# Fused co-attention and expert kernel: DMA transposes of two or three pieces, six fp16 piece buffers, constant matmuls ahead of the expert blocks, a down block between at the switch

## The reference

```python
c  = layernorm(x)
s  = (c @ w_c + b_c)[:, None] + (ctx @ w_q + b_q)[None, :] + einsum('cd,qd,d->cq', c, ctx, w_cq) + b_cq
a  = softmax(s, axis=1)
att = a @ ctx
b_att = softmax(max(s, axis=1))
q2c = b_att @ c
z  = concat([c, att, c * att, c * q2c]) @ W_l.T + b_l
x  = x + z
# mixture of 8 experts, each row goes to one
n  = layernorm(x)
e  = argmax(n @ wr + br)
x  = x + gelu(n @ w1[e] + b1[e]) @ w2[e] + b2[e]
```

## Time and profile before

| | us |
|---|---|
| median of 3 runs | 235.63 (235.04 to 236.16) |
| the profiled execution's own time | 233.51 |
| its span, first to last instruction | 231.8 |
| TensorE matmul busy | 198.0 (85%) |
| VectorE busy | 180.0 (78%) |
| ScalarE busy | 158.0 (68%) |
| POOL busy | 130.5 (56%) |
| DMA queue of SP, share of 16 engines' span | 93.2% |

### The profile page before, as it was taken

One profiled execution on the slowest core, in us unless ns is written; L12 is line 12 of the kernel. 1 busy time (PEld: TensorE's weight loads), 2 busy tenths in 40 slices (PEclk: granted clock), 3 DMA queues, 4 the chain that ended last, 5 costly groups with the idle time before them and its releaser, 6 DMA issues.

```text
span 231.8 us, 5012 instructions
## 1 busy us (share of the span) xinstructions
PE 198.0 (85%) x1837; PEld 148.7 (64%) x1837; DVE 180.0 (78%) x393; ACT 158.0 (68%) x249; POOL 130.5 (56%) x179
## 2 busy tenths in 40 slices
PE   0298798995999969999999999899993799799970
PEld 0133356663676736776866767789983799789960
DVE  2789997995997994997997998958847447567770
ACT  2750799994799689399699699689432355667630
POOL 4699405999607987505906988654400740037783
PEclk9999999999999988999999999999995579999997
DMA  6999999899999999999989999969992459999200
GB/s 206 382 277 247 192 298 244 182 221 201 262 193 254 226 203 226 267 170 243 245 193 261 209 204 225 212 141 210 237 285 78 146 200 296 370 365 382 71 21 0
DMA packets 141918, 51.25 MB, mean 221 GB/s; under 512 B 121156, under 2 KB 139733, under 8 KB 141894
## 3 DMA queue, kind: packets, MB, share of 16 engines
q1 hardware_dynamic: 140960, 49.56, 93.2%
q0 software_dynamic: 784, 1.38, 1.7%
q10 hardware_dynamic: 150, 0.00, 0.0%
HBM read 10.22 MB, written 3.75 MB: 60 GB/s over the span
## 4 chain that ended last, share of the span: by engine, by line
PE 42%; DVE 22%; DMA 12%; issue 11%; ACT 9%; POOL 3%; DVEq 0%; ACTq 0%; POOLq 0%
DMA PT<-Phl 10%; DVE S L792 5%; PE psX L1075 5%; PE psS L1055 5%; PE psS L1057 5%; PE psS L1056 5%; ACT S L646 5%; DVE Phl L809 4%; PE psO L1075 4%; ACT Phl L661 3%; PE psS L1288 3%; PE psX L1077 3%; POOL out_x L603 2%; PE psS L1274 2%; PE psO L1077 2%
## 5 line engine op out<-in xcount | busy, mean ns | idle before, releaser
L646 ACT ACTIVATE S<-S,negb 128x1024 f32<-128x1024 f32 x48 | 55.0, 1145 | 14.6 <-DVE negb L800 14.6
L792 DVE TENSOR_SCALAR_CACHE_REDUCE S<-psS 128x1024 f32<-128x1024 f32 x48 | 58.2, 1216 | 8.2 <-PE psS L1057 7.7
L809 DVE TENSOR_TENSOR Phl<-S,Phl 128x1024 f16<-128x1024 f32 x38 | 50.9, 1340 | 7.7 <-ACT Phl L661 7.6
L661 ACT CAST Phl<-S 128x1024 f16<-128x1024 f32 x48 | 50.2, 1045 | 6.1 <-DMA PT<-Phl 4.7
L533 POOL TENSOR_TENSOR Phl<-S,Phl 128x256 f16<-128x256 f32 x40 | 26.2, 685 | 48.6 <-ACT Phl L661 48.6
L1055 PE MATMUL psS<-qT,gh 128*128 128x512 f16 x96 | 37.8, 394 | 3.3 <-DVE gl L769 2.7
L1075 PE MATMUL psO<-qn,PT 128*128 128x256 f16 x204 | 37.4, 277 | 2.5 <-DMA PT<-Phl 2.4
L1075 PE MATMUL psX<-qn,PT 128*128 128x256 f16 x204 | 36.4, 273 | 2.6 <-DMA PT<-Phl 2.6
L1056 PE MATMUL psS<-qT,gh 128*128 128x512 f16 x96 | 37.7, 392 | 0.0
L1057 PE MATMUL psS<-qT,gl 128*128 128x512 f16 x96 | 37.7, 392 | 0.0
L1077 PE MATMUL psO<-qn,PT 128*128 128x128 f16 x204 | 36.0, 222 | 0.0
(11 more groups left out here) (239 smaller groups left out, 424.9 us busy)
## 6 DMA issues: line engine op xcount, KB each, us to landing
PT<-wp SPq DMA_DIRECT2D x8, 512.0 KB, 4.9
stageT<-in_ctxT SPq DMA_DIRECT2D x6, 512.0 KB, 7.3
qn<-wp SPq DMA_DIRECT2D x6, 512.0 KB, 6.8
wp<-in_w SPq DMA_DIRECT2D x4, 512.0 KB, 4.8
stageT<-in_w SPq DMA_DIRECT2D x4, 512.0 KB, 4.7
rows_by_expert<-stageT SPq DMA_DIRECT2D x4, 385.5 KB, 5.3
PT<-Phl SPq DMA_TRANSPOSE x48, 4.1
S<-rows_by_expert SPq DMA_DIRECT2D x2, 258.0 KB, 5.6
```

Source lines behind the costliest of these rows:

```text
L646: nc.scalar.activation(slot(t, e), slot(t, e), ACT.Exp, bias=negb[:, t:t + 1], accum_out=Lp[:, t * NG + e:t * NG + e + 1]).then_inc(exp_do ...
L661: nc.scalar.copy(hi, slot(t, e)).then_inc(high_done, 1)
L792: nc.vector.tensor_scalar(out=into, in0=bank(u, n)[:, 0:into.shape[1]], scalar1=1.0 / GS, scalar2=None, op0=ALU.mult, op1=ALU.max, accum_o ...
L809: nc.vector.tensor_tensor(lo, slot(t, e), hi, ALU.subtract).then_inc(low_done, 1)
```

## The change

- A DMA transpose takes a unit of pieces: (0,1), (2,3) and (4,5,tail); for the last tile (0,1), (2,3), (4), (5,tail). The context rows likewise go as (0,1), (2,3), (4,5), (tail). Semaphores `pT_landed` and `qn_landed` count units.
- `Phl` holds all six full pieces and the tail in one row, so a piece has its own place and ScalarE waits in `high` for the unit of the tile before. To fit, the descriptor scratch of POOL's DMAs is 8192 bytes instead of the default (16384).
- On SP's queue, two w1 loads stand ahead of the context transposes; the w2 loads stand behind the last unit of tiles 1 to 4.
- `x_re`: ScalarE copies x early, POOL adds the bias behind its low part of tile 1.
- `fill(n)`: n matmuls of 512 columns on a constant, into a PSUM bank that nobody reads: 2 ahead of the rank matmuls, 12 behind them.
- At b = 6, `down(6)` stands behind `turn(0)` and ahead of `up(8)` instead of behind `turn(1)`.

```diff
-        Phl = sb("Phl", [P, PARTS, 2, GR], F16)
-        Ptail = sb("Ptail", [P, 2, TAILP], F16)
+        PW = 2 * GR
+        Phl = sb("Phl", [P, (NG - 1) * PW + 2 * TAILP], F16)
+        Ptail = Phl[:, (NG - 1) * PW:].rearrange("p (a w) -> p a w", a=2)
...
+        QN_UNITS = ((0, 2), (2, 4), (4, 6), (6, 7))
...
+        def pT_units(t):
+
+            return ((0, 2), (2, 4), (4, 5), (5, NG)) if t == T - 1 else ((0, 2), (2, 4), (4, NG))
...
-            def transpose(t, e):
-
-                wait_low(sp, t, e)
+            def transpose(t, g):
+
+                e0, e1 = pT_units(t)[g]
+                for e in range(e0, e1):
+                    wait_low(sp, t, e)
                 if t > 0:
-                    sp.wait_ge(pv_done, (t - 1) * NG + e + 1)
-                src, _, _, dst = piece(t, e)
-                sp.dma_start_transpose(dst, src).then_inc(pT_landed[e], 16)
+                    sp.wait_ge(pv_done, (t - 1) * NG + e1)
+                end = (NG - 1) * PW + 2 * TAILP if e1 == NG else e1 * PW
+                n = len([j for e in range(e0, e1) for j in tiles(e)])
+                sp.dma_start_transpose(PT[:, 2 * e0 * TW:2 * (e0 * TW + n), :],
+                                       Phl[:, e0 * PW:end]).then_inc(pT_landed[g], 16)
...
-            for k in range(H - 1):
-                load_w1(k)
+            load_w1(0)
+            load_w1(1)
+            for g, (n0, n1) in enumerate(QN_UNITS):
...
+            load_w1(2)
...
+            for t in range(T):
+                for g in range(len(pT_units(t))):
+                    transpose(t, g)
+                if t == 0:
+                    load_w1(H - 1)
+                elif t <= H:
+                    load_w2(t - 1)
...
-            nc.gpsimd.tensor_tensor(x_re, x_sb, blr[:, :].unsqueeze(1).broadcast_to([P, T, D]),
-                                    ALU.add).then_inc(x_re_ready, 1)
...
             low_piece(1, 3)
+            pool.wait_ge(x_kept, 1)
+            pool.wait_ge(late_landed, 16 * NLATE)
+            nc.gpsimd.tensor_tensor(x_re, x_re, blr[:, :].unsqueeze(1).broadcast_to([P, T, D]),
+                                    ALU.add).then_inc(x_re_ready, 1)
...
             deviation(2, H, T)
+            act.wait_ge(qTl_ready, DVE_LOW.index(4) + 1)
+            act.wait_ge(qTl_pool_ready, POOL_LOW.index(5) + 1)
+            nc.scalar.copy(x_re, x_sb).then_inc(x_kept, 1)
...
-                past = t * (NG - 1) + e - PARTS
-                if e == NG - 1 and t > 0:
-                    act.wait_ge(pT_landed[e], 16 * t)
+                if t > 0:
+                    act.wait_ge(pT_landed[pT_unit(t - 1, e)], 16 * t)
...
-                pe.wait_ge(pT_landed[e], 16 * (t + 1))
+                pe.wait_ge(pT_landed[pT_unit(t, e)], 16 * (t + 1 if t < T - 1 or e < 5 else 1))
...
+            filler = ones[:, :].bitcast(F16)
+
+            def fill(n):
+
+                for _ in range(n):
+                    nc.tensor.matmul(psS[2][:, 0:CH], filler[:, 0:P],
+                                     filler.unsqueeze(1).broadcast_to([P, 2, 2 * P]), start=True, stop=True)
...
             linear_c(2)
+            fill(2)
...
             last.then_inc(ranks_in_psum, 1)
+            fill(12)
...
                 if b == E - 2:
                     turn(0)
+                    down(b)
...
                 if b == E - 2:
                     turn(1)
-                down(b)
+                else:
+                    down(b)
```

More of the change, by code:

```diff
@@ L67, in build @@
     SLOTS = 8
-    PARTS = 4
     BANKS = 3
@@ L204, in build @@
         qT_landed = [sem(f"qT_landed{n}") for n in range(NG)]
-        qn_landed = [sem(f"qn_landed{n}") for n in range(NG)]
+        qn_landed = [sem(f"qn_landed{g}") for g in range(4)]
         late_landed = sem("late_landed")
@@ L228, in build @@
         exp_done = sem("exp_done")
-        pT_landed = [sem(f"pT_landed{e}") for e in range(NG)]
+        pT_landed = [sem(f"pT_landed{g}") for g in range(4)]
         high_done = sem("high_done")
@@ L320, in columns, with qn_unit, pT_unit @@
             return buf[:, 0, 0:w], buf[:, 1, 0:w]
+        QN_UNITS = ((0, 2), (2, 4), (4, 6), (6, 7))
+        def qn_unit(n):
+            return min(n // 2, 3)
         def rows_of(n):
-            k = len(tiles(n))
-            buf = qT[:, n, :, :] if n < NG - 1 else qTend[:, :, :]
-            return buf.rearrange("p a w -> p (a w)"), qn[:, 2 * n * TW:2 * n * TW + 2 * k, :]
+            return qn[:, 2 * n * TW:2 * n * TW + 2 * len(tiles(n)), :]
+        def pT_units(t):
+            return ((0, 2), (2, 4), (4, 5), (5, NG)) if t == T - 1 else ((0, 2), (2, 4), (4, NG))
+        def pT_unit(t, e):
+            return [e0 <= e < e1 for e0, e1 in pT_units(t)].index(True)
         def pool_low(t, e):
@@ L349, in bank, with piece @@
             return psS[(u * NG + n) % BANKS]
[L351 to L356, removed]
+        def piece(e):
+            w = cols(e, GR)[1] - e * GR
+            buf = Phl[:, e * PW:(e + 1) * PW].rearrange("p (a w) -> p a w", a=2) if e < NG - 1 else Ptail
+            return buf[:, 0, 0:w], buf[:, 1, 0:w]
         def block_w(b):
@@ L402, in load_w2 @@
                              w2[k * n:(k + 1) * n].rearrange("e (k p) d -> p e k d", p=P)).then_inc(w_landed[H + k], 16)
-            for k in range(H - 1):
-                load_w1(k)
+            load_w1(0)
+            load_w1(1)
+            for g, (n0, n1) in enumerate(QN_UNITS):
+                for n in range(n0, n1):
+                    sp.wait_ge(qTh_ready, n + 1)
+                    if n in DVE_LOW:
+                        sp.wait_ge(qTl_ready, DVE_LOW.index(n) + 1)
+                    else:
+                        sp.wait_ge(qTl_pool_ready, POOL_LOW.index(n) + 1)
+                src = qT[:, n0:n1, :, :].rearrange("p n a w -> p (n a w)") if n1 < NG else \
+                    qTend[:, :, :].rearrange("p a w -> p (a w)")
+                k = sum(len(tiles(n)) for n in range(n0, n1))
+                sp.dma_start_transpose(qn[:, 2 * n0 * TW:2 * (n0 * TW + k), :], src).then_inc(qn_landed[g], 16)
+            load_w1(2)
             for r in (0, 32):
@@ L529, in low_piece @@
                 pool.wait_ge(high_done, t * NG + e + 1)
-                _, hi, lo, _ = piece(t, e)
+                hi, lo = piece(e)
                 for a in range(0, GR, CHUNK):
@@ L1072, in weighted @@
                 n, acc = len(tiles(e)), psA[t % 2]
-                both = rows_of(e)[1].rearrange("p (a j) d -> p a j d", a=2)
+                both = rows_of(e).rearrange("p (a j) d -> p a j d", a=2)
                 for i, j in enumerate(tiles(e)):
```

39 lines of the change are left out of this document (9 added, 30 removed).

## The result

The changed kernel takes 251.31 us (median of 4, 249.56 to 251.76) against 235.66 for the one before: ratio 1.0652, 95% interval 1.0595 to 1.0709. Slower was forecast, by 4.6 us; it is 15.7. The profiled execution took 251.76 us with a span of 250.0, 18.2 more than the span of before, whose execution was 2.1 under its median.

What follows compares the result with a forecast made beforehand. TensorE was taken to set the pace in attention. Attention +5.4, slow landings +1.5, constant matmuls -1.6 and switch -0.7 gave +4.6 us on the median of 235.6: 240.2, rounded to 240, range 231 to 245.

Steps and rivals of the forecast that it cites:

- the wait for the third unit: Attention: pieces 4, 5 and tail land 6.2 us after the tail's low part; TensorE waits 1.1 to 1.4 us each round.
- slow landings: Attention transposes that land late, like one of 6.3 us with no load ahead: +1.5 us, between nothing and 5.
- to the third round: Attention up to 62.18 us: ScalarE's 3.16 us stall goes, waits for pairs come; 1.0 us gained, 1.5 earlier start included.
- third to fifth round: Two attention rounds of 17.9 us against 35.7 together: +0.1 us; a 2.23 us hole goes, waits come.
- fifth to eighth: Three attention rounds, each 1.3 us longer: +4.0 us.
- last tiles: End of attention: tile 6's unit lands 2.8 us late, TensorE has 0.4 us of slack: +2.3 us.
- experts and switch: After attention: -1.6 us from the constant matmuls and -0.7 us from moving down(6).
- rival C: Waits in attention also cost the clock: 245 to 249 us with three slow landings at 1.5 us; chance 0.06.
- the start: Before attention: with x + bias moved off POOL's early work, L747 is short and the first exponentials come 1.5 us earlier.
- The waits of 1.2 and 0.8 us: TensorE's waits at the two units after its first pair, before the third round: 2.0 us together.
- constant matmuls: Ahead of ranks and expert blocks: full clock gives -2.8 us, delays cost 1.2: -1.6 us, bounds -2.8 to +1.8.
- the switch: Expert blocks: down(6), 0.7 us, fills TensorE's 1.44 us hole in front of VectorE's L977: -0.7 us.

Runs made afterwards that it cites:

- runs 1 and 2: The changed kernel with each probability piece transposed by itself, 230.58 us; and with units (0,1), (2,3), (4,5), (tail) for all tiles, 240.02 us.
- the shifted one: The changed kernel with 32 constant matmuls of 8 columns at the start of TensorE's program: 247.22 us, ratio 1.0489; its repeat, one execution, 245.8 us.

## Why the prediction was wrong in size

The direction and the wait for the third unit were right. The price of slow landings and of the clock was not, and the expert blocks had pauses that nothing before showed. By the terms of its sum, in the profiled executions, forecast and measured:

| term | forecast | measured |
|---|---|---|
| to the third round | -1.0 | +1.9 |
| third to fifth round | +0.1 | +2.1 |
| fifth to eighth | +4.0 | +7.4 |
| last tiles | +2.3 | +3.9 |
| slow landings (in the four above) | +1.5 | - |
| experts and switch | -2.3 | +2.9 |
| sum | +4.6 | +18.2 |

**What held.** The third unit is late in every round from the one at 64 us on: landing 6.2 to 6.4 us behind the first tile, where no read is in it, for a forecast of 6.1, pairs 5.6 to 5.8 for 5.4, issue 0.14 us behind the tail's low part, waits of 1.06 to 1.26 for 1.1 to 1.4, and quiet rounds of 17.87 and 17.85 for 17.8 to 17.9. The rule that a DMA is issued early and waited for late (the Trainium skill, DMA: Bandwidth & Descriptors, Rules for kernel authors) is borne out by runs 1 and 2. Merging cost time here, and the pieces, of 524,288 bytes, are not the small transfers that the same section of the Trainium skill would have coalesced. The 25 transposes of probabilities are there, and ScalarE's cast waits for no landing. The halved scratch cost nothing that a scatter shows: the shortest pause stays 0.30 us. VectorE's L747 (L761 here), beside which POOL no longer works, is short, as forecast (1.70 us before, 0.16 now, and 0.16 in all fifteen profiles with the copy against 1.23 to 2.33 in the five without), though it comes 1.1 us later than the 21.38 of before:

```profile
22.51 0.16 DVE L761 TENSOR_TENSOR sc<-rstd 128x4 f32<-128x4 f32 x1
```

**The step that failed first: "For landings such as the 6.3 I add 1.5 ... most landings being quiet".** The term for slow landings was taken at the low side. Two third units of seven meet an instruction read and take 7.75 and 8.40; the one at 102 gave 2.0 us by itself. What holds such a landing was in the trace of before: a read of 16 KB of instructions starts at 100.3, inside the landing of 6.3 us that the prediction couldn't explain, and one lies in each of the two late landings that it put down to a load (7.29 and 7.46 us, reads at 53.3 and 82.8). Behind a load without such a read, pieces landed in 5.44 and 6.01 us. The first pair costs too, with a load ahead and a read in it (8.84, wait of 0.98 us, a round of 18.5).

**The second: the clock, rival C, which had 0.06 and stood at nothing in the sum.** It was weighed as something for three slow landings together. One wait of 3.10 us sufficed (3.41 us at half speed, 1.7 lost), so did the first wait of the kernel, 4.50 us where the steps gave 3.4 (6.83 us from 1.4 us before its end on, TensorE busy for 5.40 of it, 2.7 lost), and the waits of 1.80 and 1.73 us in the last tiles (3.42 us, 1.7 lost). Length alone doesn't tell: before, the wait of 2.23 us at 85.05 was followed by 3.41 us at 0.50, the one of 2.37 at 56.34 by none. Of the 2.9 us missing to the third round the start has 1.1: the first exponential comes 0.4 earlier, not 1.5, since VectorE's work ahead was later in this profile. Over all profiles it comes at 28.8 in the mean of five without the copy and at 27.8 of fifteen with it, so the term is -1.0. The waits of 1.2 and 0.8 us that were to follow didn't come.

**The third: constant matmuls.** "The blocks behind then run at full clock" is right, and nothing was delayed: -3.0 us from the first up to the switch on a chip without pauses, more than the -1.6 taken. With pauses the stretch is 15.9 to 18.5 us, longer than the 15.06 of before, whose profile has none. No row of before could show them. They are nearly all of the change from 247.7 to 251.8 us in one and the same program: 6.4 us more in the stretch, less the 1.7 behind it.

**The fourth: the switch.** -0.7 was forecast on "VectorE stands ahead of L977". From the switch to the last down block the changed kernel takes 28.8 us, before 29.1: -0.3. Profiles with pauses and the edit have 28.4 to 28.8 (four), those without the edit 29.1 to 29.4 (three). Without pauses TensorE comes to the third batch of rows before it has landed, and the gain is given back there.

Without the pauses the changed kernel was at 247.7 in its one execution, 7.7 us above the forecast, and that remainder lies in attention: slow landings and the clock behind the waits.

**Left open.** What the pauses are: no DMA or semaphore in the records ends them, and only that they go with the chip or the time of the measurement was seen. In each of the six profiles that have pauses and the constant matmuls, a read of 16 KB of instructions starts between 1.0 us before and 0.4 us behind the end of the last pause (204.95 and 204.58 in the first profile after). That points at the supply of instructions, which no run tested. How the 8.1 us of waits for pairs divide between loads and instruction reads was not taken apart. No version is shown to beat the kernel before on every chip: with single units and the rest of the change it is 0.980 to 0.989 on two chips without pauses, and 0.997 (to 1.0001) on one with them. With the old places of the loads it is 0.998 to 1.000 on two.

## What to carry to other kernels

A transfer that is merged with a later one inherits the later one's start; look for the piece that is ready last and for the consumer that comes first, and count from there. When the merged landing becomes what a round waits for, whatever else holds it (a load ahead, an instruction read) is paid in full, and the clock may go with it. A gain ahead of a transfer that a later step waits for is worth nothing until that transfer is earlier too.

## What the runs showed of the hardware

- A read of 16 KB of instructions that falls into a transpose of 38 blocks makes it land at 7.37 to 8.68 us instead of 6.14 to 7.06 (11 against 31 landings). In a repeat of the changed kernel the same two units are hit again; in that of the shifted one, one of two.
- The same program pauses 0.2 to 1.1 us at a time in the middle of a row of 128-column matmuls on some chips and not on others: four programs have profiles of both kinds. With the constant matmuls it is 3.9 to 6.4 us on top of a stretch of 12.1.
- TensorE's granted clock was 0.50 for 3.4 us behind a single wait of 3.1 us, and for 6.8 us from the last 1.4 us of a wait of 4.5 us on. In the kernel before it was 0.50 for 3.4 us behind a wait of 2.23 us and stayed at 1.00 behind one of 2.37.
